# A two-stage graph kernel on one core: the first load of stage 2 goes ahead of stage 1's last visit, and its first steps are prepared inside it

## What is computed

```
x = layernorm(x + A @ (exp(-evals * t)[:, None] * (A.T @ x)))            # the spectral layer
x = layernorm(x + tanh(((A + I) / rowsum(A + I)) @ (x @ W) + b))         # the graph layer
```

## Time and profile before

| | us |
|---|---|
| three executions | 629.28, 629.96, 630.16 |
| median | 629.96 |
| profiled execution | 632.82 |
| its span | 630.7 |

### The profile page before, as it was taken

The page is one execution under the profiler, slowest core; times in us unless marked ns, Lnnn a source line. Parts: engine busy times, 40 slices in busy tenths (PEclk is TensorE's granted clock), DMA queues, the critical chain, the costliest instruction groups (busy, mean ns, idle before and its releaser), DMA issues.

```text
span 630.7 us, 8071 instructions
## 1 busy us (share of the span) xinstructions
PE 590.4 (94%) x2486; PEld 451.3 (72%) x2486; DVE 515.1 (82%) x604; ACT 396.3 (63%) x859; POOL 364.4 (58%) x206
## 2 busy tenths in 40 slices
PE   6999999999996789999999999999999969999992
PEld 5878788778774566667888888888888847655561
DVE  4789989988887999698879889596776576989992
ACT  4899999999986644545565655545443454445552
POOL 0000000000131988877999999778886779796961
PEclk9999999999999799999999999999999989999997
DMA  8999999999999999999987999298994499999201
GB/s 285 386 387 386 386 387 387 387 387 387 386 331 328 280 301 252 287 266 272 317 220 198 263 280 302 60 264 204 247 251 133 128 346 296 345 332 296 58 18 50
DMA packets 141305, 174.67 MB, mean 277 GB/s; under 512 B 6868, under 2 KB 105428, under 8 KB 141272
## 3 DMA queue, kind: packets, MB, share of 16 engines
q1 hardware_dynamic: 88992, 121.68, 61.3%
q10 hardware_dynamic: 52280, 52.58, 30.6%
HBM read 172.13 MB, written 2.11 MB: 276 GB/s over the span
## 4 chain that ended last, share of the span: by engine, by line
PE 69%; POOL 9%; DVE 6%; ACT 5%; DMA 4%; issue 3%; SPq 1%; ACTq 1%; POOLq 0%; DVEq 0%
PE ps L759 13%; PE ps L761 13%; PE ps L760 13%; PE ps L735 7%; POOL lo L409 7%; PE ps L736 6%; PE ps L737 6%; PE ps L755 6%; DMA raw<-in_adj_dram 4%; ACT hi L445 3%; DVE vt L596 3%; PE ps L824 1%; PE ps L827 1%; POOL rstd L401 1%; ACT hi L460 1%
## 5 line engine op out<-in xcount | busy, mean ns | idle before, releaser
L409 POOL TENSOR_TENSOR lo<-vt,hi 128x1024 fp32r<-128x1024 f32 x129 | 326.7, 2559 | 59.1 <-ACT hi L460 58.2
L596 DVE STREAM_TRANSPOSE vt<-raw 128x1024 f32<-128x1024 f32 x184 | 222.2, 1226 | 62.9 <-PE ps L761 52.4
L460 ACT ACTIVATE hi<-vt 128x1024 fp32r<-128x1024 f32 x163 | 169.6, 1061 | 111.3 <-DVE vt L596 93.1
L579 DVE TENSOR_TENSOR lo<-raw,hi 128x1024 fp32r<-128x1024 f32 x124 | 153.5, 1240 | 21.3 <-ACT hi L445 20.7
L445 ACT ACTIVATE hi<-raw 128x512 fp32r<-128x512 f32 x256 | 158.2, 621 | 14.2 <-DMA raw<-in_adj_dram 4.8
L391 POOL TENSOR_TENSOR lo<-raw,hi 128x1024 fp32r<-128x1024 f32 x4 | 10.7, 2685 | 180.8 <-ACT hi L445 180.8
L759 PE MATMUL ps<-hi,s_hi 128*128 128x512 f32 x232 | 99.1, 427 | 9.5 <-issue 5.2
L735 PE MATMUL ps<-hi,xg_hi 128*128 128x512 f32 x256 | 102.0, 399 | 2.7 <-DVE lo L579 1.4
L736 PE MATMUL ps<-lo,xg_hi 128*128 128x512 f32 x256 | 99.9, 390 | 0.0
L737 PE MATMUL ps<-hi,xg_lo 128*128 128x512 f32 x256 | 99.8, 390 | 0.0
L759 PE MATMUL ps<-hi,p_hi 128*128 128x512 f32 x206 | 89.1, 433 | 7.0 <-POOL lo L409 7.0
(11 more groups left out here) (66 smaller groups left out, 512.9 us busy)
## 6 DMA issues: line engine op xcount, KB each, us to landing
raw<-in_adj_dram SPq DMA_DIRECT2D x63, 1024.0 KB, 14.2
raw<-in_adj_dram SPq DMA_DIRECT2D x90, 512.0 KB, 9.3
raw<-in_adj_dram ACTq DMA_DIRECT2D x88, 512.0 KB, 11.6
late_raw<-in_adj_dram SPq DMA_DIRECT2D x8, 512.0 KB, 11.6
late_raw<-in_adj_dram ACTq DMA_DIRECT2D x8, 512.0 KB, 14.3
xn<-in_x_dram SPq DMA_DIRECT2D x8, 256.0 KB, 12.2
x_sb<-in_x_dram SPq DMA_DIRECT2D x8, 256.0 KB, 13.1
out_dram<-x_sb ACTq DMA_DIRECT2D x8, 256.0 KB, 3.0
```

Source lines behind the costliest of these rows:

```text
L409: nc.gpsimd.tensor_tensor(lo[:, slot(p), :], vt[:, slot(p), :], hi[:, slot(p), :].bitcast(f32), ALU.subtract).then_inc(pool_lo_ready, 1)
L460: nc.scalar.activation(hi[:, slot(s), :], vt[:, slot(s), :], ACT.Copy).then_inc(hi_ready, 1)
L579: nc.vector.tensor_tensor(lo[:, q % RING1, :], raw[:, k, 2 * h:2 * h + 2, :].rearrange("p r n -> p (r n)"), hi[:, q % RING1, :].bitcast(f3 ...
L596: nc.vector.transpose(vt[:, slot(s), :].rearrange("p (m a i) -> p m a i", m=2, a=RB), load_buffer(st.load).rearrange("p (a m e i) -> p e m ...
```

## The change

It does five things.

- **Load 0 goes early.** It gets a buffer of its own, `early_raw`, in the place that `x_sb` takes later. SP issues all four quarters before the first chunk of the last visit. Load 4 takes over the raw buffers that load 0 would have left free, so loads 1 to 4 go where 0 to 3 went, and from load 5 on every load waits for the same turn as before. The rows of x for group 0 are loaded behind load 4, when step 3 is turned.
- **Steps 0 and 1 are turned and split inside the last visit.** VectorE turns them behind chunks 5 and 6, ScalarE rounds them behind chunks 6 and 7.
- **TensorE does `products(0)` and `products(1)` ahead of `spectrum(3)`.**
- **GpSimd takes six halves of the last visit**, q = 1, 3, 5, 7, 9 and 11, in place of 1, 5, 9 and 13.
- **The spectrum's steps are set in another order.** The turns 2 to 5 go between VectorE's `s_lo` blocks; blocks 6 and 7 of `s_hi` and all of `full` move behind hi steps on ScalarE, and `full` has a semaphore of its own.

```
+    EARLY = BUFS3
...
-        buf = min(free_at, key=free_at.get)
+        buf = min(free_at, key=free_at.get) if n else EARLY
...
-    LATE_POOL = [q for q in range(PAIRS) if q % 4 == 1]
-    LATE_DVE = [q for q in range(PAIRS) if q % 4 != 1]
+    LATE_POOL = [1, 3, 5, 7, 9, 11]
+    LATE_DVE = [q for q in range(PAIRS) if q not in LATE_POOL]
...
+            load_quarters(sp, 0, (0, 2, 1, 3))
             visit1(LAST, None, LAST)
-            for n in range(NL):
+            for n in range(1, NL):
...
+                if n == NU:
+                    sp.wait_ge(vturned, LAST_STEP[0] + 1)
+                    sp.dma_start(x_sb[:, 0, :], x_v[0, 0]).then_inc(x_in[0], 16)
```

ScalarE's part:

```
+            for k in range(NK):
+                chunk1(LAST, k)
+                if k == 4 or k == 5:
+                    spectrum_hi(k - 4)
+                if k == 4 or k == 6:
+                    first_load(k // 2 - 1)
+                if k == 6:
+                    hi_step(0)
+            hi_step(1)
+            first_load(3)
+            for k in (2, 3):
+                spectrum_hi(k)
+            first_load(4)
+            hi_step(2)
+            spectrum_hi(4)
+            hi_step(3)
+            spectrum_hi(5)
...
-            for p in range(AHEAD, POSITIONS):
+            for p in range(4, POSITIONS):
                 if p < STEPS:
                     hi_step(p)
+                if 6 <= p + 2 < NK:
+                    spectrum_hi(p + 2)
+                if WHOLE_FROM <= p < NK:
+                    spectrum_full(p)
```

VectorE's part, without the rest of its spectrum, whose new order the rows below show:

```
+            for k in range(NK):
                 for h in range(2):
-                    if i < NK and 2 * i + h in LATE_DVE:
-                        half1(LAST, i, h)
+                    if 2 * k + h in LATE_DVE:
+                        half1(LAST, k, h)
+                if k >= 2:
+                    spectrum_out(k - 2)
+                if k == 4 or k == 5:
+                    spectrum_lo(k - 4)
+                if k == 5 or k == 6:
+                    turn_step(k - 5)
...
-                if p + AHEAD < STEPS:
+                if 6 <= p + AHEAD < STEPS:
                     turn_step(p + AHEAD)
```

TensorE's part:

```
+            products(0)
+            products(1)
             spectrum(NU - 1)
```

122 lines of the change are left out of this document (68 added, 54 removed).

## The result

| | before | after |
|---|---|---|
| median of four executions, taken in turn on one chip | 630.06 us | 642.96 us |
| lowest and highest | 629.28, 631.64 | 640.21, 645.04 |
| profiled execution, its span | 632.82, 630.7 | 645.04, 642.9 |

The ratio is 1.0198, with a 95% interval of 1.0161 to 1.0235: the change makes the kernel 2% slower. The forecast was 633.3 us, in a range of 628.8 to 638.2. The sign was right and the size was not; the time lies outside the range.

A forecast was written before the change was run, and what follows sets the result against it. Load and TensorE limits lie together in stage 1, the load leading; step 7's shift was taken as the kernel's. Terms +5.4 +1.4 +1.3 -4.8 = +3.3 us on the 629.96 us median gave 633.3 us, range 628.8 to 638.2.

The forecast's parts named there:

- what step 7 gains or loses is the kernel's gain or loss: After stage 2's step 7 TensorE waits for GpSimd only 1.6 us up to 500 us, so its shift reaches the end.
- (a): Early load ahead of visit 7, stage 1's last: 2.10 MB at 348 GB/s delays TensorE's first chunk, +5.4 us (4.8 to 7.0).
- the shift of step 7: How much later TensorE starts stage 2's step 7, the sum of all terms: +3.3 us.
- (b): Visit 7 from its first chunk up to E: chunks 0 to 3 +1.4 us, chunks 4 to 7 +1.3 us.
- The walk: Stepping through each stretch's new order of work with durations from the earlier trace, to get the terms.
- third rival: VectorE's and GpSimd's splits slow each other, all six odd halves overlapping an even one: +2.9 us, 636.2 us; chance 0.15.
- (c): From E to stage 2's step 7: TensorE waits go, step 3 is late next; 21.5 instead of 26.3 us, -4.8 us.
- E: Moment TensorE starts the third group of spectrum transposes, all chunks done: 197.52 us before, forecast 205.6.
- the wait before step 3: TensorE idles 7 us for VectorE's lo of stage 2's step 3, then runs at half clock, 1.9 us lost.
- (d): Parts said to cost nothing: load 4's new buffer, loads 1 to 4, x rows of group 0, moved `full` copies.
- The first: Rival: cover is worth more than the load costs, clock stays up, ring hides GpSimd's halves; -1.4 us, 628.6; chance 0.14.
- The second, taken up later: Rival: no change; TensorE's later GpSimd waits absorb the delay, +1.2 us or less, 629 to 631; chance 0.18.

The follow-up runs named there:

- order: Kernel before the change with only the lists at the end of stage 1 reordered, no early load or moved buffer: 630.85 us, ratio 0.9983.
- wide1k: Changed kernel with the early load as four 512 KB transfers to all 128 partitions in 1 KB pieces: 636.21 us, ratio 1.0097 to before.
- late01: Changed kernel with ScalarE's hi of steps 0 and 1 moved later, so GpSimd's lo of them runs behind VectorE's last halves: 647.76 us.
- lo3: Changed kernel with VectorE's lo of step 3 moved directly behind its turn of step 4: 644.79 us, ratio 1.0198 to before.
- rot: Kernel before the change with only load 0 in the extra place and the buffers moved, load 0 at its old time: 630.59 us, ratio 0.9998.
- fine: Changed kernel with the early load as 16 transfers of 128 KB in turn to the four quarters, instead of four of 512 KB: 641.48 us.

## Why the prediction was right and wrong

**What bounds the kernel.** Right that load and TensorE bound stage 1 together and that TensorE is late by all of a load delay but about 0.6 us: the first chunk was read 13.8 us late and TensorE came to it 13.3 us late. Wrong in half of the sentence that what step 7 gains or loses is the kernel's gain or loss. It holds for losses. For gains `order` refutes it: the view of TensorE's waits from 223.5 us on the earlier trace rows shows who waits now, not who would wait if all came earlier. VectorE's 1.46 us for load 8 at 257.47 was the row to read.

**(a), the early load: the step that failed.** +13.3 us instead of +5.4, outside its bounds of 4.8 to 7.0; it is 7.9 of the 12.1 us by which the shift of step 7 was missed. The mechanism was right as far as it went (the load takes its time out of a full pipe, and TensorE gets the delay), and with whole-width transfers the load costs the 6.0 us that were forecast (wide1k). The mis-sized factor was the rate: 221 GB/s for its own pieces, and less still where they mixed with whole chunks. "348 GB/s, from the window in which the same shape of transfer has a full backlog": the shape was the same, but there two queues carried complementary quarters, and here one queue carried them in a row. The sentence "The trace shows no such load alone on one queue" passed over 209.9 to 212.4 us, where such quarters, with rows of x among them, move at 168 GB/s; by that rate the first chunk is 12.5 us late and the term 11.9 us. The bounds came from whole chunks (387) and from a stretch with both queues at work (276), and neither holds for one queue with quarters.

**(b), visit 7.** +5.3 instead of +2.7, outside the bounds' sum of 0.5 to 4.7. The walk was right as far as it went (30.1 us in late01, 29.8 forecast). What it left out is the contention of the two splitters, the prediction's third rival at +2.9, measured at 2.3. The rival had the place wrong: the odd halves beside the even ones cost next to nothing, and GpSimd's halves of steps 0 and 1 beside VectorE's last two cost all of it. It was given as an alternative with a chance of 0.15; it belonged into the sum, since these halves lie beside each other in the order itself.

**(c), E to step 7.** -3.2 instead of -4.8, at the edge of its bounds (-6.5 to -3). The chain was as told: no wait between the transposes, step 3 late next with 6.32 us (7 forecast) released by VectorE's lo, half clock behind it (granted clock 0.50 from 228.94 to 235.77, 1.2 GHz). Step 3 came at E+15.6 instead of E+14.1, and that is the difference: the walk had one wait of VectorE for ScalarE's s_hi, and there were two. The first, 1.42 us, comes from what the walk put at nothing, ScalarE's issue of load 4's quarters, which held its hi of step 2 back to 220.20, 2.1 us behind the turn, and with it the s_hi behind it; TensorE waited 3.02 us before step 2 for the same reason. In wide1k that issue ended at E+2.9 instead of E+4.0, the first wait was 0.33 us, step 3 came at E+14.5 and the term was -4.5. VectorE, after:

```profile
222.33 1.12 DVE L665 SCALAR_TENSOR_TENSOR s_lo<-ps,coef,s_hi 128x128 fp32r<-128x128 f32 x4 [1.42 <-ACT s_hi L493]
...
229.26 1.12 DVE L665 SCALAR_TENSOR_TENSOR s_lo<-ps,coef,s_hi 128x128 fp32r<-128x128 f32 x4 [1.37 <-ACT s_hi L493]
230.30 1.39 DVE L637 TENSOR_TENSOR lo<-vt,hi 128x1024 fp32r<-128x1024 f32 x1
```

What was not in it either: removing the wait before step 3 alone brings under 1 us (lo3).

**(d)** Right for the moved buffers and x's later load: rot shows that they cost nothing. What load 4 does cost, ScalarE's time to issue it, stands under (c).

**The rivals.** The first (faster, 628.6) rested on E moving by less than 6 us; it moved by 18.6. The third is the one that happened, beside the mis-sized load. The second, taken up later, did not happen: from step 7 to 500 us the lag went from 15.4 to 15.9 us.

**The signs.** Of the signs named, four came as told (a wait on VectorE's lo before the first chunk, half clock there, none between the transposes, the wait before step 3), and three were out by the size of (a): 180.95 instead of 173, E at 216.12 instead of 204 to 207, step 7 at 239.21 instead of 226 to 229.

**What stays open.** Why fine gained so little is not settled: whether a transfer must be over on all engines before the next begins was not tried by itself. Nor was it tried how many transfers must be outstanding before ScalarE's issue takes long, nor what lets three executions of order come out below 628.

## What to carry to other kernels

Price a transfer by its own shape on its own queue: if it lands on a quarter or a half of the partitions, look for a place in the trace where such transfers run without a partner, and do not take the rate of two queues that complete each other. Count the transfers in front and behind as slowed too. Ask what an engine that issues transfers has to do behind them. Before work is pulled ahead of a point, look at what waits behind that point for something else than the engine you relieve, here VectorE for load 8; a gain reaches the end only if the next supplier has slack too. A tiny transfer in a full queue can be the dearest one in it: move tables with pieces of a few bytes to a stretch where the stream has slack.
